# A graph-layer kernel whose VectorE, ScalarE and TensorE loops are written out with constant columns, slots and wait values

## The reference

```
h = max(layernorm(x), 0)
neigh = segment_sum(h[src], dst)                     # layer 0
x = x + relu(relu(((1 + eps) * h + neigh) @ W1 + b1) @ W2 + b2)
h = max(layernorm(x), 0)
W_r = sum_b coefficients[r, b] * bases[b]            # layer 1, 16 relations
out = h @ w_self.T;  out[src] += h[dst] @ W_type
x = x + out
```

## Time and profile before

| | |
|---|---|
| three runs | 1557.21 us median, 1554.61 to 1560.56 |
| the profiled execution, its own time | 1555.58 us |
| its span | 1553.6 us |
| instructions recorded | 20,995 |
| mean granted clock of TensorE | 0.769 of 2.4 GHz |
| first mixed loop | 78 to 205 us |
| second | 237 to 439 us |
| third | 485 to 818 us |
| middle part | 818 to 940 us |
| last loop | 940 to 1545 us |

### The profile page before, as it was taken

One profiled execution on the slowest core, in us unless ns is written; L12 is line 12 of the kernel. 1 busy time (PEld: TensorE's weight loads), 2 busy tenths in 40 slices (PEclk: granted clock), 3 DMA queues, 4 the chain that ended last, 5 costly groups with the idle time before them and its releaser, 6 DMA issues. The chain is left out here.

```text
span 1553.6 us, 20995 instructions
## 1 busy us (share of the span) xinstructions
PE 976.2 (63%) x4924; PEld 672.7 (43%) x4925; DVE 696.7 (45%) x2173; ACT 395.2 (25%) x936; POOL 848.3 (55%) x829
## 2 busy tenths in 40 slices
PE   3635833767942395878698995166565655656576
PEld 2512421333521163555474444155454544545455
DVE  5824883545786384677595431022122222222224
ACT  6313712334510273556383430000000000000000
POOL 0275457576357676668600006566666666666662
PEclk9656975898975597998798997576776767666767
DMA  3432212222212222222302892111111111111113
GB/s 79 133 78 59 47 32 78 56 70 61 41 28 64 61 60 67 66 62 65 61 1 68 260 291 84 43 46 44 46 44 46 44 44 48 43 45 44 47 44 58
DMA packets 47251, 103.20 MB, mean 66 GB/s; under 512 B 15485, under 2 KB 26382, under 8 KB 46800
## 3 DMA queue, kind: packets, MB, share of 16 engines
q0 software_dynamic: 33024, 67.69, 17.8%
q1 hardware_dynamic: 13846, 33.16, 6.9%
q10 hardware_dynamic: 308, 1.60, 0.4%
HBM read 71.73 MB, written 30.65 MB: 66 GB/s over the span
## 5 line engine op out<-in xcount | busy, mean ns | idle before, releaser
L370 POOL DMA_INDIRECT gathered<-h_table,row_of x418 | 461.2, 1103 | 311.7 <-issue 114.0
L370 POOL DMA_INDIRECT gathered<-z_table,row_of x405 | 386.2, 954 | 367.4 <-DMA z_table<-spare 164.8
L821 PE MATMUL ps<-gathered,node_hot 128*125 128x128 f32 x1620 | 349.5, 361 | 252.6 <-issue 234.7
L821 PEld LDWEIGHTS ps<-gathered,node_hot 128*125 128x125 f32 x1620 | 297.1, 261 | 305.1 <-issue 303.6
L435 ACT ACTIVATE place_val_b<-place_hot,code_b 125x128 f16<-125x128 f16 x728 | 314.4, 518 | 440.8 <-DVE place_hot L619 308.1
L653 DVE TENSOR_SCALAR node_hot<-iota_f,key_of 128x250 f32<-128x250 f32 x405 | 135.5, 373 | 470.2 <-remote 283.1
L826 PE MATMUL ps<-node_hot,gathered 128*128 128x506 bf16 (+1 forms) x1254 | 249.0, 344 | 96.9 <-issue 95.5
L802 PE MATMUL ps<-chunk_hot,place_val_a 125*128 125x405 f16 (+2 forms) x728 | 211.5, 319 | 102.3 <-issue 93.0
L804 PE MATMUL ps<-chunk_hot,place_val_b 125*128 125x405 f16 (+2 forms) x728 | 209.5, 316 | 41.7 <-issue 38.4
L826 PEld LDWEIGHTS ps<-node_hot,gathered 128*128 128x128 bf16 x1254 | 125.4, 102 | 204.2 <-issue 139.9
L623 DVE TENSOR_SCALAR chunk_hot<-iota_h,chunk_f 125x405 f16<-125x405 f16 (+2 forms) x728 | 168.5, 309 | 28.4 <-issue 28.4
(11 more groups left out here) (133 smaller groups left out, 335.2 us busy)
## 6 DMA issues: line engine op xcount, KB each, us to landing
z_table<-spare SPq DMA_DIRECT2D x50, 448.0 KB
gathered<-h_table,row_of POOLq DMA_INDIRECT x418
gathered<-z_table,row_of POOLq DMA_INDIRECT x405
z_table<-spare SPq DMA_DIRECT2D x50, 52.0 KB
out<-x_sb SPq DMA_DIRECT2D x6, 224.0 KB
h_table<-gathered SPq DMA_DIRECT2D x1, 1092.0 KB
w_table<-spare SPq DMA_DIRECT2D x2, 512.0 KB
w_rel<-w_table SPq DMA_DIRECT2D x1, 1024.0 KB, 4.9
```

Of the source, the lines that this page charges most:

```text
L370: pool.indirect_dma_start(place if s == LAST else place.rearrange("p j d -> p (j d)"), None, z_table if s == LAST else h_table, bass.Indir ...
L821: last = T.matmul(psf[0:NP, bass.ds(offs[i] + half * D, D)], node_hot_of[s][:, k % HOTS[s], half * NP:(half + 1) * NP], gathered_of[s][:, ...
```

## The change

All `Fori` loops of DVE, ACT and PE go. The rounds become loops of the program that writes the kernel, so each round has its own instructions, with constant columns, slots, ring places and wait values. Order and number of matmuls, one-hots, activations, gathers and DMAs stay; no buffer and no wait is added or dropped. In the changed kernel lines from 262 on have smaller numbers (L653 becomes L641, L821 becomes L809).

```diff
-        def batches_alone(engine, s, sort_batch, first, last):
-
-            turns = (last - first) // BATCH_BUFS
-            if turns:
-                with engine.Fori(0, turns) as r:
-                    for b in range(BATCH_BUFS):
-                        sort_batch(s, r * BATCH_BUFS + (first + b), (BATCHES_BEFORE[s] + first + b) % BATCH_BUFS)
-            for b in range(first + turns * BATCH_BUFS, last):
+        def batches_alone(s, sort_batch, first, last):
+
+            for b in range(first, last):
                 sort_batch(s, b, (BATCHES_BEFORE[s] + b) % BATCH_BUFS)
...
-                with engine.Fori(r0, r1) as r:
-                    for g in range(GROUPS[s]):
-                        group_work(s, g, r)
...
+            for r in range(BESIDE_ROUNDS[s + 1]):
+                if r == mid:
+
+                    batches_alone(s + 1, sort_batch, mid * per_round, mid * per_round + alone)
+                taken = r * per_round + (alone if r >= mid else 0)
+                for g in range(GROUPS[s]):
+                    group_work(s, g, r)
...
-                                         scale=code_b[l][:, bass.ds(batch * BATCH + (c0 + i), 1)]).then_inc(val_ready, 1)
+                                         scale=code_b[l][:, c0 + batch * BATCH + i:c0 + batch * BATCH + i + 1]).then_inc(val_ready, 1)
...
-                run = bass.ds(batch * BATCH + c0, BATCH)
+                run = slice(c0 + batch * BATCH, c0 + (batch + 1) * BATCH)
...
-                                    chunk_f[l][:, bass.ds(batch * BATCH + (c0 + i), 1)], None, ALU.is_equal)
+                                    chunk_f[l][:, c0 + batch * BATCH + i:c0 + batch * BATCH + i + 1], None, ALU.is_equal)
...
-                                    key_of[s][:, bass.ds(r * RING[s] + k, 1)],
+                                    key_of[s][:, r * RING[s] + k:r * RING[s] + k + 1],
...
-                    bucket_off[s][0:1, bass.ds(r * GROUPS[s] + g, 1), 0:GROUP[s]].rearrange("p g i -> p (g i)"),
+                    bucket_off[s][0:1, r * GROUPS[s] + g:r * GROUPS[s] + g + 1, 0:GROUP[s]].rearrange("p g i -> p (g i)"),
```

More of the change, by code:

```diff
@@ L274, in batches_alone, with rounds_beside @@
                 sort_batch(s, b, (BATCHES_BEFORE[s] + b) % BATCH_BUFS)
-        def rounds_beside(engine, s, group_work, sort_batch, between=None):
+        def rounds_beside(s, group_work, sort_batch):
             mid, per_round, alone = ALONE_ROUND[s + 1], PER_ROUND[s + 1], ALONE[s + 1]
[L279 to L286, removed]
-                with engine.Fori(r0, r1) as r:
-                    for g in range(GROUPS[s]):
-                        group_work(s, g, r)
-                        b0, b1 = (min(n, GROUPS[s] - 1) * per_round // (GROUPS[s] - 1) for n in (g, g + 1))
-                        for b in range(b0, b1):
-                            sort_batch(s + 1, r * per_round + (taken + b), (BATCHES_BEFORE[s + 1] + taken + b) % BATCH_BUFS)
@@ L295, in rounds_rest @@
[L295 to L301, removed]
+            for r in range(BESIDE_ROUNDS[s + 1]):
[4 more added lines that the diff above has]
+                    group_work(s, g, r)
+                    b0, b1 = (min(n, GROUPS[s] - 1) * per_round // (GROUPS[s] - 1) for n in (g, g + 1))
+                    batches_alone(s + 1, sort_batch, taken + b0, taken + b1)
@@ L303, in build, with rounds_rest @@
+        def rounds_rest(s, group_work):
+            for r in range((BESIDE_ROUNDS + [0])[s + 1], ROUNDS[s]):
+                for g in range(GROUPS[s]):
+                    group_work(s, g, r)
         block = ctx.enter_context(nc.Block())
@@ L435, in sort_batch @@
                     nc.scalar.activation(place_val_b[:, buf, i, :], place_hot[:, buf, :, i], ACT.Copy,
-                                         scale=code_b[l][:, bass.ds(batch * BATCH + (c0 + i), 1)]).then_inc(val_ready, 1)
+                                         scale=code_b[l][:, c0 + batch * BATCH + i:c0 + batch * BATCH + i + 1]).then_inc(val_ready, 1)
             for s in range(1, NSORT):
-                batches_alone(nc.scalar, s, sort_batch, 0, COLS[s] // BATCH)
+                batches_alone(s, sort_batch, 0, COLS[s] // BATCH)
             def z_odd_copies(tiles):
@@ L705, in _ @@
                     dve.wait_ge(nhot_used, RING[0] + CHUNKS_BEFORE[s - 1])
-                rounds_beside(nc.vector, s - 1, node_hots, sort_batch)
+                rounds_beside(s - 1, node_hots, sort_batch)
                 read_sorted(s)
                 decode(s)
-                rounds_rest(nc.vector, s - 1, node_hots)
+                rounds_rest(s - 1, node_hots)
                 if s < LAST:
@@ L754, in _ @@
             V.tensor_copy(wsT[:, :], ps[:, 7, 0:D]).then_inc(wsT_ready, 1)
-            rounds_rest(nc.vector, LAST, node_hots)
+            rounds_rest(LAST, node_hots)
             dve.wait_ge(nhot_used, RING[0] + sum(CHUNKS))
@@ L854, in _ @@
             for s in range(1, NSORT):
-                rounds_beside(nc.tensor, s - 1, add_up, sort_batch)
-                rounds_rest(nc.tensor, s - 1, add_up)
+                rounds_beside(s - 1, add_up, sort_batch)
+                rounds_rest(s - 1, add_up)
                 if s < LAST:
@@ L920, in _ @@
                          skip_group_check=True)
-            rounds_rest(nc.tensor, LAST, add_up)
+            rounds_rest(LAST, add_up)
 _INS = ["x", "src", "dst", "edge_type_16", "L0_gnn_eps", "L0_gnn_W1", "L0_gnn_b1", "L0_gnn_W2", "L0_gnn_b2",
```

## The result

The changed kernel takes 1543.5 us (median of four runs, 1540.7 to 1547.5) against 1558.6 us for the kernel before (four runs, 1554.6 to 1560.6): 0.9916 of it, 95% interval 0.9888 to 0.9944. It is faster by a little under 1% (13 us by this ratio, 15 us by the medians), inside the range. The likeliest case had promised 79 us. The experiments ran on five chips, one after the other. On the first two, and in the runs above, the kernel before took 1544 to 1559 us; on the last three it took 1320 to 1322 us. A single execution of 1565 us on a free chip, at a granted clock of 0.549, is a slow one of another kind and is left out of all ratios.

What follows compares the result with a forecast made beforehand. PE and DVE instructions were taken to pass in bulk only in POOL's pauses, 69 per us. Removing 5,506 saves 79 us, other terms zero: 1555.6 - 79 = 1476.6, plus 1.6 for the median, 1478 us; range 1424 to 1548 us.

Steps and rivals of the forecast that it cites:

- The likeliest case: Forecast as worked out: 5,506 fewer register instructions shorten POOL's pauses by 79 us, giving 1478 us; chance 0.47.
- What bounds the kernel: Loops with gathers: PE and DVE instructions pass in bulk only when POOL pauses; PE's matmuls then run at 23 times the pace.
- The rate: Mixed and last loops: about 17,990 instructions pass in 259 us of POOL's pauses, 69 per us.
- Their own 32 to 60 ns: Register instructions' own durations on DVE, ACT and PE: zero, being covered; 93 us on PE should that cover go.
- The maxima of 700 ns on register instructions: DVE's and PE's register instructions are seen held for 700 ns like the others, the reason given for taking 79 us.
- The turns of the loops: DVE's 1.57 us gap behind a turn, five turns in the mixed loops: 8 us at the most, taken as zero.
- Longer code: PE's stream grows from 5,111 to 11,314 instructions, 24 more blocks of code to fetch: taken as zero.
- Rival 3: Mixed and last loops: PE's written-out code comes too late, 58 us for 24 blocks; 1615 or 1574 us; chance 0.11.
- Rival 2: Register instructions are free, lying under the queued matmuls; the change gives within 8 us of 1557 us; chance 0.07.
- Rival 1: Only PE's stream counts, in the loops with gathers: 41 us go, giving 1516 us; chance 0.20.
- rival 4: More than the proportion: the stall works like an overflowing store; half of 259 us of pauses goes, 1427 us; chance 0.15.
- The forecast is wrong as a whole if the instructions drop by a quarter and POOL's pauses stay: Sign against the forecast, which expected about 15,500 instructions and POOL's pauses in the four loops near 180 us instead of 259.

Runs made afterwards that it cites:

- free chip: One of the last three chips, where the kernel before the change took 1320 to 1322 us.
- held chips: The first two chips, where the kernel before the change took 1544 to 1559 us.
- dve_loops: Changed kernel, except that DVE (VectorE) keeps its loops; held chip: 1545.6 us, 1.0007 of the kernel before.
- again: The changed kernel unaltered, run again on a free chip: 1316.4 us, 0.9959 of the kernel before.

## Why the prediction was wrong

**What bounds the kernel.** "One resource that every instruction of PE and DVE passes, and that POOL's gathers take while they are issued" is half right. On held chips PE is slow beside gathers by index and only there (14 matmuls in 33 us; 260 beside SyncE's transfers; 305 beside nothing; the 23 times in the prediction are 22). But gathers do not do this of necessity: the same code, with the same gathers at the same pitch, runs 100 matmuls in the same 33 us on a free chip. And it is not every instruction of DVE: one-hots without a register instruction run eight in 2.02 us while PE is held.

**The rate, and with it the 79 us.** This is the step that failed. 17,990 instructions in 259 us of pauses was a division of two totals, not a price. Taking 5,506 off was to shorten the pauses by 79 us; the trace has 5,314 fewer, and the pauses went from 259 to 248. Halving PE's work in the last loop gave 250 instructions per us of pause or more, and PE's 1,678 register instructions put back left the pauses there at 73 us, as without them. With the pauses cut up in four ways they stayed at 69 to 84 us, some 0.17 to 0.21 us per gather, and depended only weakly on what PE does. That the quotient lay between 37 and 53 per us in each of four loops looked like support; but no loop of that trace differs from another in its instructions alone. Per gather the last loop has half the operations (9.1, against 18.3 to 21.0) and also half the pause (0.24 us, against 0.40 to 0.51), and it also differs in having no batches, another table and another ring. What sets the pause per gather is not shown.

**Their own 32 to 60 ns.** Zero was right: with 1,551 extra instructions on DVE the ratio on free chips is 0.995 and 0.996, without them 0.996 and 0.997, and PE's own come back for some 5 us on a held one.

**The maxima of 700 ns on register instructions** were read as their being held for themselves. For DVE the traces bear this out: the same one-hot comes once per 1.4 us with a register instruction in front and eight times in 2.02 us without. What did not follow is the price. The 40 us of idle time in front of these operations went, and 13 us of the kernel's time. On PE the register instructions that are left have a maximum of 51 ns where they had 711, and PE is held beside them as before (14 matmuls in 33 us). There those durations were a companion of the hold and no sign of who pays for it.

**The turns of the loops.** Taken as zero, with 8 us as a bound. DVE's loops are what costs: 0.9929 with the loops on ACT alone, 1.0007 with them on DVE, and the gap of the earlier trace rows is gone. But a loop brings turns and register instructions, and how the 13 us divide is not measured. The idle time of DVE behind the five turns of the kernel before is 1.57, 1.36, 1.83, 1.10 and 1.19 us, 7 us in all. Its idle time in front of the chunk one-hots and `place_val_a`, none of them behind a turn, is 39.8 us before and 30.1 us in `dve_loops`. That some of it reaches PE shows there: PE stands 15.9 us, up to 512.5 us, for the `place_val_a` behind the eight slow one-hots. On free chips 3 to 5 us are left of the gain; which part of the change brings them was not tried.

**Longer code.** Zero was right: 45 packets of 16 KB came in (44 forecast), and PE's idle time is 0.0 in written-out code beside no gathers, and 0.0 in front of line 792 over the whole of `again`:

```profile
L792 PE MATMUL ps<-chunk_hot,place_val_b 125*128 125x405 f16 (+2 forms) x728 | 193.6, 298 | 0.0
```

Rival 3 falls, as the Trainium skill (Runtime: NRT & Kernel Launch, Instruction fetch mechanics) has it for straight lines.

**The rivals.** Rival 2, within 8 us of 1557 us and given 0.07, was nearest, though 13 us is beyond its 8: PE's register instructions cost little (some 5 us), but DVE's on a held chip are not free to DVE. Rival 1 (41 us) has the wrong engine, and with rival 4 (130 us) it falls with the rate. "The forecast is wrong as a whole if the instructions drop by a quarter and POOL's pauses stay" is what happened.

**What stays open.** What holds PE, and the register instructions of DVE, in the held runs, and whether it belongs to the chip or to the time. It goes together with the loss of semaphore updates from the trace, and every timed execution here was recorded. The Trainium skill (NOTIFIC — the notification-queue block, Overflow: three behaviours, one of which stalls the engine) says that the block which writes such records pushes back on its producers inside rather than lose one. If that push is the hold, it is an effect of recording, and an unrecorded run on a held chip would take some 1310 us; this is a guess that no run here tests, since none is unrecorded. Two things speak against it as it stands. The held trace lacks two thirds of the updates, so records are lost somewhere, if not inside that block. And beside SyncE's transfers on a held chip 6,542 updates in 220 us are in the trace, 30 per us, with PE at full pace. How much time DVE's register instructions cost while held, and whether fewer one-hots or nearly no matmuls would end the pauses, is open too, since the kernels for it met free chips three times.

## What to carry to other kernels

A quotient of two totals (instructions over pauses) is no price until one of them has been moved alone; two kernels, one with half of the matmuls and one with none of the gathers, would have shown it. "Issue" idle time that no wait explains, beside "remote" waits in a kernel on one core, may belong to the chip, the time or the recording and not to the kernel, so look at a second chip before planning against it: here it was worth 235 us, and the whole change 3 to 15. Writing loops out pays little where the engine's queue is ahead. And when one engine's stall goes away, ask who was waiting for that engine: here DVE's one-hots lost 40 us of stall and the kernel 13 us of time, with PE held as before.

## What the hardware showed that was not expected

The same program takes 1545.7 us in the held group and 1310.4 us in the free one, with the same DMA packets and the same gathers of 950 ns. TensorE's granted clock in the three mixed loops is 0.75, 0.81 and 0.81 held and 0.93, 0.95 and 0.95 free: where PE is busier it got more. While held, PE starts its instructions, and DVE those with a register instruction in front, mostly in steps that are multiples of about 0.70 us (of the 160 steps between 1 and 12 us from one weight load to the next in the changed kernel's last loop, 115 lie within 0.07 us of a multiple, where 32 would by chance). From the timeline of the changed kernel, weight loads of PE:

```profile
973.81 0.28 PEld L809 LDWEIGHTS ps<-gathered,node_hot 128*125 128x125 f32 x1 [2.51 <-issue]
977.31 0.28 PEld L809 LDWEIGHTS ps<-gathered,node_hot 128*125 128x125 f32 x1 [3.21 <-issue]
979.41 0.28 PEld L809 LDWEIGHTS ps<-gathered,node_hot 128*125 128x125 f32 x1 [1.82 <-issue]
981.51 0.28 PEld L809 LDWEIGHTS ps<-gathered,node_hot 128*125 128x125 f32 x1 [1.82 <-issue]
```

The steps are 3.50, 2.10 and 2.10 us, which is 5, 3 and 3 times 0.70, and the one-hots of `dve_loops` above lie 1.40 and 1.41 us apart, twice 0.70. PE gets fast again only some time after POOL has stopped, and stays fast after POOL has gone on: in the changed kernel a gather ends at 1111.4 us, the matmuls run close together from 1114.2 to 1122.1 us, and POOL has gone on at 1115.3 us. And three small POOL instructions behind each gather cost nothing on a held chip: it is their sum of pauses that counts there, and two thirds of their 0.46 us fell where POOL would have stood in any case.
